# Four transformer layers on one core: a new dispatcher that decides per engine, and layer-norm roots as a power on GpSimd

## The chip, the cores and the metric

The kernel runs on one core of a Trainium2 chip. The metric is the device time of one execution in microseconds (us). The core has five engines with a program each: PE (TensorE, matmuls), DVE (VectorE), ACT (ScalarE), POOL (GpSimd) and SP (SyncE, which here only issues transfers). Each engine runs its own program strictly in order and waits on semaphores for the others, so an instruction that waits also holds everything that stands behind it on its engine.

## What is computed

Two sequences (batch 2) of 1024 tokens with 256 features go through four layers, each with its own weights. All layers have the same skeleton; `_ln` is a layer norm without learned shift, and `mod` stands for the shift, scale and gate vectors that a conditioning vector gives.

```python
h = _ln(x) * (1 + scale) + shift          # layer norm 1 of 3
x = x + gate * (self_attention(h) @ W_o)  # 16 heads of 16
h = _ln(x) * (1 + scale) + shift          # 2 of 3 (in L1 a plain _ln, and no gate)
x = x + gate * (cross_attention(h, context) @ W_co)   # 77 context tokens
h = _ln(x) * (1 + scale) + shift          # 3 of 3
x = x + gate * mlp(h)                     # 256 -> 1024 -> 256
...
def _ln(x):
    m = x.mean(-1, keepdims=True)
    v = ((x - m) ** 2).mean(-1, keepdims=True)
    return (x - m) * jax.lax.rsqrt(v + EPS)
```

L0 has a mask over all 1024 x 1024 scores, L1 and L3 attend to all tokens, L2 attends in windows of 128 tokens and, in its cross attention, keeps only the 16 highest scores of the 77 (top-k). The MLP of L2 is a SwiGLU, the others are GELUs.

## The kernel before

Tokens are held in blocks of 512 (two per sequence), heads in groups. Scores of a query tile go through the PSUM ring `ring_a` (2 places) for their row maximum, which DVE takes, and are then computed again, transposed, in `ring_b` (3 places) for the exponential, which ACT takes; `ring_c` holds the products with V. Intermediate tensors travel through DRAM (`scr_q`, `scr_k`, `scr_out`, `scr_recip`).

The order of all work is fixed before the program is built. `plan()` describes the work as some dozens of coroutines ("threads") that ask for steps with `do(kind, ph, ...)`. `ph` lists the step's phases, an engine and an assumed duration each, for instance PE and then DVE; `lat` is the assumed latency of a transfer. A thread has a rank (tables `RANK`, `SECOND`, `LATER`), buffers are handed out by `Slots`, and `LINK` is the assumed time of a hand-over. `Plan.run` repeatedly takes the step that can begin first, or one of lower rank that could begin within `REACH` of it or would be wanted soon on a later phase's engine (`YIELD`). `emit` then books all phases of the step at once, each behind what has already been booked on its engine. The list `p.steps`, in the order of booking, is the order of the programs of SP, ACT, DVE and POOL. For PE alone, `play` goes through the list a second time and makes an order of its own, `pe_order`, and in a third pass it puts numbers of filling matmuls into the places where it expects PE to wait.

Those fills are products of an identity matrix with 256 columns that nothing reads (L1318 and L1322). Their number is the expected wait in us, less a margin, times 0.8 (L1318) or 0.7 (L1322), divided by `FILL_ONE` = 0.11.

A layer norm of one block is the steps `stats` and `norm` on DVE and two steps `turn` (PE transposes at L1336, ACT writes `h_feat` at L1570). `stats` is four BN_STATS (L1672), four BN_AGGR (L1675) and `inverse_root` (L1635 to L1645): fourteen operations on 128x4 numbers, each waiting for the one ahead. `norm` is four TENSOR_SCALAR (L1682) into `x_norm`, of which there is one buffer. There are 48 of them: 4 layers of 3, for 2 sequences of 2 blocks. POOL splits the row maxima into three bf16 parts (L1882 to L1885) and sends them to the query ring (L1890), prepares the top-k exponents (L1896 to L1899), multiplies gates into weights (L1864) and adds biases to the residual (L1874).

## Time and profile before

| | us |
|---|---|
| median of 3 runs (3001.68 to 3004.83) | 3004.18 |
| span of the profiled execution, first to last instruction | 3001.3 |
| PE busy, filling matmuls included | 2791.8 |
| DVE busy | 2002.4 |
| ACT busy | 1400.1 |
| POOL busy | 638.6 |

The span is that of one profiled execution; it lies within the range of the three runs, and 2.9 us below their median. Busy time is the time in which an engine had at least one instruction under way. A matmul's busy time is its latency, so the times of single groups on PE overlap at their edges and add up to more than PE's. The kernel's line numbers are written L1322.

### The profile page before, as it was taken

What the parts mean: (1) busy time and instruction counts of PE and PEld (TensorE: products, weight loads), DVE (VectorE), ACT (ScalarE), POOL (GpSimd) and SP (SyncE); (2) the same over time, 40 slices, a digit from 0 to 9 for tenths busy, and PEclk for the clock granted to TensorE, in tenths of its full rate; (3) what the DMA queues carried; (4) which work ended last, traced back from release to release, by engine and by line L of the source; (5) the groups of instructions that cost most, each with busy time, mean ns of one, the idle gap of its engine ahead of it and who ended that gap; (6) DMA issues with size and microseconds to landing.
All of it is one profiled execution on the core that took longest, in us unless ns stands there. A gap on an engine that the chain in (4) does not pass through costs nothing.

```text
span 3001.3 us, 48815 instructions
## 1 busy us (share of the span) xinstructions
PE 2791.8 (93%) x15447; PEld 1384.9 (46%) x15447; DVE 2002.4 (67%) x4848; ACT 1400.1 (47%) x2571; POOL 638.6 (21%) x967
## 2 busy tenths in 40 slices
PE   8999999999999998999988888889799999999899
PEld 5533344335536324334465566666553433333556
DVE  7778387643683865884355669677888694886631
ACT  3255635663453663664635233322225355577341
POOL 2010011221410110131124435424321000112220
PEclk9999999999999999999999999999999999999899
DMA  7323122322551312243166415531232042123521
GB/s 208 103 66 121 47 64 78 107 66 85 155 164 41 92 50 75 68 131 94 40 191 184 132 49 175 155 89 35 94 103 57 15 128 51 44 58 100 180 92 37
DMA packets 268160, 286.87 MB, mean 96 GB/s; under 512 B 70665, under 2 KB 207243, under 8 KB 267275
## 3 DMA queue, kind: packets, MB, share of 16 engines
q1 hardware_dynamic: 256651, 282.28, 32.0%
q8 instruction: 136, 2.23, 0.3%
q0 software_dynamic: 11264, 1.46, 0.3%
q14 instruction: 109, 0.89, 0.1%
HBM read 167.43 MB, written 114.72 MB: 94 GB/s over the span
## 4 chain that ended last, share of the span: by engine, by line
PE 68%; DVE 13%; issue 7%; DMA 5%; POOL 2%; ACT 2%; SPq 2%; DVEq 0%; ACTq 0%; POOLq 0%
PE ring_c L1491 11%; PE ring_b L1458 11%; PE ring_a L1414 10%; PE ring_a L1526 7%; PE ring_b L1514 6%; PE ring_b L1457 4%; PE ring_a L1503 3%; PE ring_b L1371 3%; DVE row_max L1776 2%; PE ring_a L1514 1%; DMA reciprocals<-scr_recip 1%; PE ring_a L1386 1%; DMA q_ring<-neg_max_parts 1%; PE ring_b L1485 1%; PE ring_b L1336 1%
## 5 line engine op out<-in xcount | busy, mean ns | idle before, releaser
L1599 ACT ACTIVATE probs<-ring_b 128x512 f32<-128x512 f32 (+1 forms) x1728 | 904.8, 604 | 498.0 <-PE ring_b L1458 434.8
L1776 DVE TENSOR_REDUCE row_max<-ring_a 128x1 f32<-128x1024 f32 x512 | 600.1, 1219 | 130.5 <-PE ring_a L1414 127.6
L1458 PE MATMUL ring_b<-q_ring,k_ring 100*128 100x512 bf16 x1536 | 514.0, 381 | 20.9 <-ACT probs L1599 4.8
L1414 PE MATMUL ring_a<-k_ring,q_ring 96*128 96x512 bf16 x1536 | 450.8, 383 | 21.0 <-issue 3.8
L1491 PE MATMUL ring_c<-probs,v_and_ones 128*17 128x512 f32 x3072 | 400.9, 599 | 5.3 <-ACT probs L1599 4.8
L1882 POOL CAST neg_max_parts<-neg_max 16x128 bf16<-16x128 f32 x112 | 33.0, 294 | 1594.7 <-ACT neg_max L1593 1265.6
L1773 DVE CUSTOM_DVE_ANT_0 w_mlp<-ring_a,w_mlp 128x1024 bf16<-128x1024 f32 x256 | 300.6, 1221 | 53.2 <-PE ring_a L1414 52.6
L1820 DVE TENSOR_TENSOR x_tok<-x_tok,ring_a 128x512 f32<-128x512 f32 x96 | 66.0, 688 | 338.8 <-PE ring_a L1526 206.7
L1458 PEld LDWEIGHTS ring_b<-q_ring,k_ring 100*128 100x128 bf16 x1536 | 142.2, 97 | 313.3 <-issue 210.1
L1414 PEld LDWEIGHTS ring_a<-k_ring,q_ring 96*128 96x128 bf16 x1536 | 127.6, 98 | 298.8 <-issue 219.9
L1514 PE MATMUL ring_b<-h_feat,w_mlp 128*128 128x512 f32 x512 | 229.9, 597 | 3.6 <-ACT h_feat L1570 1.7
L1526 PE MATMUL ring_a<-w_mlp 128*128 128x256 f32 x1024 | 225.6, 381 | 3.1 <-issue 1.9
L1526 PEld LDWEIGHTS ring_a<-w_mlp 128*128 128x128 f32 x1024 | 194.0, 191 | 34.3 <-issue 8.3
L1457 PE MATMUL ring_b<-w_mlp 128*128 128x512 bf16 x512 | 194.4, 380 | 0.7 <-issue 0.4
L1617 ACT ACTIVATE w_mlp<-ring_b,bias_cols 128x512 f32<-128x512 f32 x128 | 87.9, 687 | 200.5 <-PE ring_b L1514 200.4
L1890 POOL DMA_DIRECT2D q_ring<-neg_max_parts x336 | 166.4, 499 | 38.1 <-POOL neg_max_parts L1885 29.8
L1779 DVE TENSOR_REDUCE row_max<-ring_a 128x8 f32<-128x616 f32 (+1 forms) x128 | 111.0, 901 | 80.1 <-PE ring_a L1424 62.0
L1583 ACT ACTIVATE raw<-ring_b,bias_cols 128x512 f32<-128x512 f32 (+1 forms) x104 | 69.1, 664 | 180.7 <-PE ring_b L1371 165.8
L1514 PEld LDWEIGHTS ring_b<-h_feat,w_mlp 128*128 128x128 f32 x512 | 96.0, 191 | 120.7 <-issue 110.8
L1593 ACT ACTIVATE neg_max<-ring_b 16x128 f32<-16x128 f32 x112 | 29.0, 260 | 244.1 <-PE ring_b L1439 244.0
L1570 ACT ACTIVATE h_feat<-ring_b,mod_cols 128x512 f32<-128x512 f32 (+1 forms) x92 | 66.3, 757 | 141.4 <-PE ring_b L1336 141.0
L1896 POOL TENSOR_SCALAR topk_marks<-topk_marks 128x616 f32<-128x616 f32 x32 | 72.6, 2269 | 272.0 <-DVE topk_marks L1801 271.7
(149 smaller groups left out, 3726.7 us busy)
## 6 DMA issues: line engine op xcount, KB each, us to landing
q_ring<-scr_q SPq DMA_DIRECT2D x128, 384.0 KB, 4.4
scr_q<-split SPq DMA_DIRECT2D x64, 384.0 KB, 2.9
k_ring<-scr_k SPq DMA_DIRECT2D x64, 384.0 KB, 5.2
scr_q<-split SPq DMA_DIRECT2D x64, 256.0 KB, 3.1
scr_out<-out_stage SPq DMA_DIRECT2D x128, 128.0 KB, 2.6
scr_out<-out_stage SPq DMA_DIRECT2D x64, 256.0 KB, 2.2
h_feat<-scr_out SPq DMA_DIRECT2D x56, 256.0 KB
reciprocals<-scr_recip SPq DMA_DIRECT2D x56, 256.0 KB
```

The costliest lines, as they stand in the source:

```text
L1371: last = mm(ps[:, 0:s.width], w[:, k, at + s.hh * P:at + (s.hh + 1) * P], src[:, k, 0:s.width], start=k == 0, stop=k == KF - 1)
L1414: last = mm(ps[:, half * BLOCK:(half + 1) * BLOCK], q[0:PARTS, h, t * P:(t + 1) * P], k_view(g)[0:PARTS, h, half * BLOCK:(half + 1) * BLOC ...
L1457: mm(ps[:, :], IDB[:], MASKT[:, s.kt, q0:q0 + BLOCK], start=True, stop=False)
L1458: last = mm(ps[:, :], k_view(g)[0:ROWS, h, s.kt * P:(s.kt + 1) * P], q[0:ROWS, h, q0:q0 + BLOCK], start=not g.masked, stop=True)
L1491: last = mm(rows, VA[:, u.kt, g.heads[tile % 2], :], probs, start=u.kt == 0, stop=u.last)
L1514: last = mm(ps[:, 0:BLOCK], w1[:, k, at:at + P], HT[:, k, s.b, s.blk * BLOCK:(s.blk + 1) * BLOCK], start=k == 0, stop=k == KF - 1)
L1526: last = mm(ps[:, t * FEAT:(t + 1) * FEAT], HID[:, k, tok:tok + P], W2[:, k, :], start=k == 0, stop=k == HIDDEN // P - 1)
L1599: f(PT[0:n, s.pt, :], ps[0:n, :], ACT.Exp, **kw).then_inc(b_evac, 1)
L1773: v.tensor_tensor_reduce(out=JUNK[:, k, :], in0=ps, in1=MASKQ[:, t, :], scale=1.0, scalar=-3.4e38, op0=ALU.add, op1=ALU.max, accum_out=NM[ ...
L1776: v.tensor_reduce(NM[:, s.nm, s.u:s.u + 1], ps, AX.X, ALU.max).then_inc(a_evac, 1)
L1779: v.tensor_reduce(NM[:, s.nm, s.u * 8:s.u * 8 + 8], ps.rearrange("p (i k) -> p i k", k=P)[:, :, 0:n], AX.X, ALU.max).then_inc(a_evac, 1)
L1890: pool.dma_start(QR[PARTS + 1 + j:PARTS + 2 + j, g.q, :], MS[:, s.ms, j, :]).then_inc(max_in[g.q], 16)
```

## The change

`Plan.run` now treats phases one by one. A step's first phase is a candidate, and so is the head of each of three queues of later phases (`a` and `b` for the rings, `c` for the rest). The engine whose candidate can begin first is chosen, and on it the candidate of lowest rank that can begin within `REACH`, which is now at most 0.2. `issue` books one phase and appends the step to `order[engine]`, so each engine, PE too, has an order of its own from one pass, and the fills are set in that pass by the formulas of before. `play`, `YIELD` and `emit` are gone. Nearly all assumed durations and latencies are new numbers, as are `RANK`, `SECOND`, `LATER`, `REACH` and `LINK`, and after a pair of PE steps of different kind around `pv` a little is added. Buffers go round in the order in which they are given back, and a step that gives one back has no assumed early time any more.

A layer norm has a step more. DVE does the statistics and signals (`stats_ready`); POOL does `root`, an addition of eps and a power of -0.5 on 128x4 numbers; DVE's `norm` waits for `root_ready`. The one root for the context tokens (77x2, once in the program) stays on DVE with its Newton steps. POOL now also waits for DVE's constants before its first instruction.

```diff
-LINK = dict(PE=0.22, ACT=0.16, DVE=0.13, POOL=0.12, SP=0.1)
+LINK = dict(PE=0.31, ACT=0.14, DVE=0.13, POOL=0.1, SP=0.0)
...
-            first, head = min(((at, t) for at, t in ready), key=lambda x: (x[0], x[1].rank))
-            eng = head.want["ph"][0][0]
-            at, t = min(((at, t) for at, t in ready if t.want["ph"][0][0] == eng and at <= first + REACH[eng]),
-                        key=lambda x: (x[1].rank, x[0]))
...
+            for q in self.queue.values():
+                if q:
+                    s, n, at = q[0]
+                    eng = s["ph"][n][0]
+                    ready.append((max(at, self.free[eng]), s["rank"], 0, None, s, n, eng))
...
+            at, _, _, _, _, _, eng = min(ready, key=lambda x: x[:3])
+            at, rank, _, t, s, n, _ = min((x for x in ready if x[6] == eng and x[0] <= at + REACH[eng]), key=lambda x: x[1:3] + x[:1])
...
-REACH = dict(PE=0.05, ACT=0.25, DVE=1.2, POOL=5, SP=0.1)
+REACH = dict(PE=0.0, ACT=0.1, DVE=0.0, POOL=0.2, SP=0.2)
...
-            s = yield do("stats", [("DVE", 4.7)], after=[src], l=l, i=i, b=b, blk=blk, src=src)
+            s = yield do("stats", [("DVE", 1.85)], after=[src], counts=["stat_n"], l=l, i=i, b=b, blk=blk, src=src)
+            s = yield do("root", [("POOL", 1.0)], after=[s], counts=["root_n"], l=l, i=i, b=b, blk=blk, of=s)
             xn, last, _ = yield ("get", "XN")
-            n = yield do("norm", [("DVE", 1.9)], after=[s, last], counts=["xn_n"], l=l, i=i, b=b, blk=blk, xs=xn, last=last)
+            n = yield do("norm", [("DVE", 1.293)], after=[s, last], counts=["xn_n"], l=l, i=i, b=b, blk=blk, xs=xn, last=last,
+                         root=s)
...
-            s = yield do("mod", [("PE", 1.75), ("DVE", 0.55)], after=[s], ring="a", l=l, i=i, n=n)
+            s = yield do("mod", [("PE", 1.68), ("DVE", 0.41)], after=[s], ring="a", l=l, i=i, n=n)
...
-                    link(last)
-                    inverse_root(RSTD[:, s.b, s.blk, 0, :], RSTD[:, s.b, s.blk, 1, :], mv[:, :, 1], LAYERS[s.l]["eps"])
+                    last.then_inc(stats_ready, 1)
                 elif s.kind == "norm":
                     if s.last is not None:
                         dve.wait_ge(b_full, s.last.bn + 1)
+                    dve.wait_ge(root_ready, s.root.root_n + 1)
...
+            pool.wait_ge(setup_dve, 1)
+            for s in whole.order["POOL"]:
...
+                elif s.kind == "root":
+                    pool.wait_ge(stats_ready, s.of.stat_n + 1)
+                    y = RSTD[:, s.b, s.blk, 0, :]
+                    link(g_.tensor_scalar(RSTD[:, s.b, s.blk, 1, :], MV[:, s.b, s.blk, :, 1], LAYERS[s.l]["eps"], None, ALU.add))
+                    g_.tensor_tensor(out=y, in0=RSTD[:, s.b, s.blk, 1, :], in1=HALF[:], op=ALU.pow).then_inc(root_ready, 1)
+                    pool.wait_ge(root_ready, s.root_n + 1)
```

Where the change moves instructions, three places show it. The first is DVE in layer L2, in the middle of the top-k (MAX and MATCH_REPLACE find the sixteen highest scores of `topk_scores`, `x_tok` is the residual). Before, the rows from one `x_norm` to the next top-k are:

```order
L1682 TENSOR_SCALAR x_norm<-x_tok,mean_var,rstd 128x256 x4
L1672 BN_STATS bn_stats<-x_tok 128x6 x4
L1675 BN_AGGR mean_var<-bn_stats 128x2 x4
L1637 TENSOR_SCALAR mean_var<-mean_var 128x4
L1638 COPY rstd<-mean_var 128x4
L1639 TENSOR_SCALAR rstd<-rstd 128x4
L1640 TENSOR_TENSOR rstd<-root_seed,rstd 128x4
L1641 TENSOR_SCALAR mean_var<-mean_var 128x4
L1643 TENSOR_TENSOR rstd<-rstd 128x4
L1644 TENSOR_TENSOR rstd<-rstd,mean_var 128x4
L1645 SCALAR_TENSOR_TENSOR rstd<-rstd 128x4
```

Two more rounds of the last three rows follow there, then the next MAX. At the like place of the changed kernel, still on DVE in L2, there is:

```order
L1764 MATCH_REPLACE topk_marks<-topk_next,topk_marks 128x77 x8
L1635 BN_STATS bn_stats<-x_tok 128x6 x4
L1638 BN_AGGR mean_var<-bn_stats 128x2 x4
L1783 TENSOR_TENSOR x_tok<-x_tok,ring_a 128x512
L1645 TENSOR_SCALAR x_norm<-x_tok,mean_var,rstd 128x256 x4
L1783 TENSOR_TENSOR x_tok<-x_tok,ring_a 128x512
```

The fourteen operations are gone, and one residual addition stands between the statistics and the `x_norm` that now needs POOL's answer. In the whole program the changed DVE order has at most two short operations or one residual pair (under 1.4 us at the mean durations of the groups of before) between the two at 22 of the 48 places, nothing at all at nine of these, and more at 26.

The second place is POOL in L2 (`neg_max_parts` are the split maxima, `topk_marks` the top-k exponents). Before:

```order
L1864 TENSOR_TENSOR w_mlp<-w_mlp,gate 128x2048
L1868 TENSOR_TENSOR gate<-gate,row_biases 128x256
L1896 TENSOR_SCALAR topk_marks<-topk_marks 128x616
L1898 TENSOR_TENSOR topk_scores<-topk_scores,topk_first 128x616
L1899 TENSOR_TENSOR topk_scores<-topk_scores,topk_marks 128x616
```

And in the changed kernel:

```order
L1828 TENSOR_TENSOR w_mlp<-w_mlp,gate 128x2048
L1838 TENSOR_TENSOR gate<-gate,row_biases 128x256
L1844 TENSOR_TENSOR x_tok<-x_tok,gate 128x1024
L1833 TENSOR_SCALAR rstd<-mean_var 128x4
L1834 TENSOR_TENSOR rstd<-rstd,minus_half 128x4
L1866 TENSOR_SCALAR topk_marks<-topk_marks 128x616
L1868 TENSOR_TENSOR topk_scores<-topk_scores,topk_first 128x616
L1869 TENSOR_TENSOR topk_scores<-topk_scores,topk_marks 128x616
```

The root stands behind a bias addition, which itself waits for an `x_norm`, and ahead of a top-k. Of the 48 roots, 11 stand right behind a bias addition, 5 right behind a top-k, 15 right behind DMA issues of the maxima, and 14 right behind another root.

The third place is PE at the start of the program (`ident_f` alone are the fills). Before:

```order
L1329 MATMUL ring_a<-cond,w_mod_or_cross_kv 128x2 x8
L1322 MATMUL ring_b<-ident_f 128x256 x46
L1336 MATMUL ring_b<-ident_f,x_norm 128x128 x8
L1322 MATMUL ring_b<-ident_f 128x256 x6
L1371 MATMUL ring_b<-h_feat,w_qkv 128x512 x2
```

And after:

```order
L1291 MATMUL ring_a<-cond,w_mod_or_cross_kv 128x2 x8
L1284 MATMUL ring_b<-ident_f 128x256 x11
L1298 MATMUL ring_b<-ident_f,x_norm 128x128 x8
L1284 MATMUL ring_b<-ident_f 128x256 x6
L1333 MATMUL ring_b<-h_feat,w_qkv 128x512 x4
```

The planner puts 11 fills instead of 46 ahead of the first transpose. Over the whole program the fills go from 2071 to 1873: 1083 to 1013 between L2's first window scores and its last top-k transpose, 652 to 633 ahead of that, 336 to 227 behind it. All other matmuls are the same in number and shape.

## Rows read from the trace of the kernel before

**Rows 1.** The page: span, busy time of each engine

```profile
span 3001.3 us, 48815 instructions
PE 2791.8 (93%) x15447; PEld 1384.9 (46%) x15447; DVE 2002.4 (67%) x4848; ACT 1400.1 (47%) x2571; POOL 638.6 (21%) x967
```

**Rows 2.** Three stretches: length, busy of PE, PEld, DVE, ACT, POOL; clock, DMA

```profile
0.00:1500.00 1500.00, 1425.69 (x7551) 626.22 (x7552) 982.68 (x1824) 782.21 (x1446) 246.12 (x449) 0.99 0.32 93
1500.00:2200.00 700.00, 601.24 (x3986) 415.75 (x3986) 500.27 (x2185) 223.55 (x384) 277.85 (x284) 0.94 0.43 125
2200.00:3000.00 800.00, 764.83 (x3912) 342.90 (x3910) 519.44 (x839) 394.32 (x741) 114.64 (x235) 0.99 0.25 75
```

**Rows 3.** Fills alone, sums over 0 to 3000: L1322, then L1318

```profile
sum 3000.00, PE 170.51 PEld 130.39; mean PE 56.84 PEld 43.46
sum 3000.00, PE 120.55 PEld 75.21; mean PE 40.18 PEld 25.07
```

**Rows 4.** The chain that ended last, share of the span by engine

```profile
PE 68%; DVE 13%; issue 7%; DMA 5%; POOL 2%; ACT 2%; SPq 2%; DVEq 0%; ACTq 0%; POOLq 0%
```

**Rows 5.** PE's waits: in total, times, longest

```profile
PE ring_b L1336 <- DVE x_norm L1682: 25.2, 12, 4.7
```

**Rows 6.** DVE's groups of the roots: busy, mean ns | idle before

```profile
L1637 DVE TENSOR_SCALAR mean_var<-mean_var 128x4 f32<-128x4 f32 x48 | 16.9, 352 | 1.6
L1638 DVE COPY rstd<-mean_var 128x4 f32<-128x4 f32 x48 | 8.7, 182 | 1.6
L1639 DVE TENSOR_SCALAR rstd<-rstd 128x4 int32<-128x4 int32 x48 | 14.2, 297 | 1.6
L1640 DVE TENSOR_TENSOR rstd<-root_seed,rstd 128x4 int32<-128x4 int32 x48 | 8.3, 174 | 1.6
L1641 DVE TENSOR_SCALAR mean_var<-mean_var 128x4 f32<-128x4 f32 x48 | 9.9, 206 | 1.6
L1643 DVE TENSOR_TENSOR rstd<-rstd 128x4 f32<-128x4 f32 x144 | 23.7, 164 | 4.9
L1644 DVE TENSOR_TENSOR rstd<-rstd,mean_var 128x4 f32<-128x4 f32 x144 | 23.7, 165 | 5.0
L1645 DVE SCALAR_TENSOR_TENSOR rstd<-rstd 128x4 f32<-128x4 f32 x144 | 23.5, 163 | 4.9
```

**Rows 7.** The chain again, in time: first root on it, one of L2

```profile
794.17 0.18 DVE mean_var L1637
...
797.25 1.39 DVE x_norm L1682 x4
...
2154.28 2.96 DVE mean_var L1637
...
2160.25 0.81 DVE topk_scores L1785
```

**Rows 8.** Timeline around the second of them: start, length, instruction

```profile
2152.69 4.52 POOL L1864 TENSOR_TENSOR w_mlp<-w_mlp,gate 128x2048 f32<-128x2048 f32 x1 [9.23 <-DVE gate L1704]
2154.28 2.95 DVE L1637 TENSOR_SCALAR mean_var<-mean_var 128x4 f32<-128x4 f32 x1
```

**Rows 9.** POOL's groups: busy, mean ns | idle before

```profile
L1896 POOL TENSOR_SCALAR topk_marks<-topk_marks 128x616 f32<-128x616 f32 x32 | 72.6, 2269 | 272.0 <-DVE topk_marks L1801 271.7
L1874 POOL TENSOR_TENSOR x_tok<-x_tok,gate 128x1024 f32<-128x1024 f32 x24 | 57.6, 2400 | 76.0 <-DVE x_norm L1682 70.5 <-ACT probs L1599 4.7
L1899 POOL TENSOR_TENSOR topk_scores<-topk_scores,topk_marks 128x616 f32<-128x616 f32 x32 | 49.1, 1535 | 2.5
L1883 POOL TENSOR_TENSOR neg_max<-neg_max,neg_max_parts 16x128 f32<-16x128 f32 x112 | 48.8, 436 | 9.4
L1898 POOL TENSOR_TENSOR topk_scores<-topk_scores,topk_first 128x616 f32<-128x616 f32 x32 | 40.7, 1272 | 2.7
L1852 POOL TENSOR_SCALAR kv_mask_col<-topk_scores 77x2 f32<-77x2 uint8 x1 | 0.5, 506 | 0.1
```

**Rows 10.** VectorE's largest constant, by the same columns

```profile
L1647 DVE MEMSET v_and_ones<- 128x2176 f32 x1 | 1.9, 1872 | 1.3 <-PEq L1986 1.3
```

510 lines of the change are left out of this document (236 added, 274 removed).

## Prediction

> **What bounds the kernel now.** I read the page first: TensorE is busy for 2791.8 of 3001.3 us, VectorE for two thirds, ScalarE for under half, GpSimd for a fifth [rows 1]. But TensorE's figure holds filling matmuls that nothing reads, so the second view is the fills alone: 170.5 us at L1322 and 120.5 us at L1318, 291 us in all [rows 3]. With the 209.5 us in which TensorE is idle (3001.3 less 2791.8), 500 us of the span are not work of TensorE. The necessary matmuls, some 2500 us, are the same before and after. All that this change can win or lose on TensorE lies in those 500 us: they are what the order of steps costs.
>
> The third view, three stretches of the span, tells where they are. Layers L0 and L1 (0 to 1500 us) leave TensorE idle for 74 us, L2 (1500 to 2200) for 99 of 700, L3 for 35 of 800. The granted clock falls to 0.94 of full speed in L2 and is 0.99 elsewhere [rows 2]. L2 also holds 142 of the 291 us of fills (122.0 and 20.3 in the same windows), so nearly half of the 500 us lies in the top-k layer, where VectorE is busy for 500 of 700 us and GpSimd is at its busiest. The fourth view, the chain that ended last, says the same: 68% TensorE, but 13% VectorE and 5% transfers [rows 4]. And in the list of waits, TensorE's largest single cause of idle is `x_norm`, the result of a layer norm: 25.2 us in 12 waits, up to 4.7 us each [rows 5].
>
> **The roots.** The change takes eight groups of operations from VectorE. Their busy time is 16.9+8.7+14.2+8.3+9.9+23.7+23.7+23.5 = 128.9 us, and the idle ahead of them, which is one operation waiting for the last, adds 22.8 us [rows 6]: 152 us for 48 roots, 3.2 us each. Most of that lies beside TensorE work and gives nothing. What counts is how many are on the chain. Walking it from start to end I find eleven of the 48, the first at 794.17 us and the longest at 2154.28 us [rows 7]. The first takes 3.08 us (794.17 to 797.25), the longest 5.97 us (to 2160.25). The eleven take 37.9 us of operations and about 3 us between them, 41 us. Seven of them are in L2.
>
> The longest is worth a look, because it shows a cost that is in no group's name: L1637, an operation on four numbers per partition, took 2.95 us, and ended within 0.05 us of the end of a GpSimd multiplication of 4.52 us that had begun ahead of it [rows 8]. VectorE was held by GpSimd. The mean of L1637 is 352 ns where its neighbours need about 165 [rows 6]. The Trainium skill (SBUF — State Buffer, "Who interferes with whom") says that a VectorE operation in a two-port mode and a GpSimd operation exclude each other for the whole instruction; the trace agrees, with the 2.95 us above. By that rule the root loses a way to be blocked on VectorE and wins one on GpSimd.
>
> In their place come two GpSimd instructions on 128x4 numbers and two hand-overs. The trace has no power operation. From below, the nearest rows are the small ones: 436 ns for 16x128, 506 ns for a TENSOR_SCALAR on two numbers per partition [rows 9], so 0.9 us for both and about 0.3 us for the hand-overs, 1.2 us. From above I take for the power what GpSimd needs for 616 elements, 2269 ns [rows 9]: 3 us in all. I take 1.2 us, as four elements per lane are much nearer to the small rows. Eleven roots then cost 13 us, not 41: 28 us less at best. As the new chain will partly run through something that was just behind, I take 25 us; the bounds are 41 (all hidden behind the VectorE work that now stands between statistics and `x_norm`) and 8 (3 us each).
>
> A rule speaks against the move: the Trainium skill (GPSIMD Engine Reference, "Engine selection") sends elementwise work to VectorE, since GpSimd is about twice as slow on two inputs. The rows show 436 ns against 165 ns per instruction, which is in that direction; but two instructions replace fourteen, so the rule would be decisive only if the power took over 2 us.
>
> **The order.** It can't be priced from a row, since every engine's order is another. What can be counted are the fills, since each stands for a wait that the planner expects, by the same formulas in both kernels. They go from 2071 to 1873, 198 fewer. At 291.06 us / 2071 = 0.1405 us each, that is 28 us. Turned back through the formulas, a fill stands for 0.11/0.8 to 0.11/0.7 us of expected wait, 0.138 to 0.157 us: 27 to 31 us. I take 29 us. This is what the new planner expects of a program with longer hand-overs from TensorE (0.31, not 0.22), so it is not flattered by optimistic links. The saving is 109 fills behind the top-k, 70 in it and 19 ahead.
>
> Part of this is the saving of the roots seen twice, because the old planner booked 4.7 us of VectorE for what is now 1.85 and a GpSimd step. I put the overlap at 15 us. Against it stand the 209.5 us of idle that no fill covers. The old formulas expect 2071 x 0.147 = 304 us of waits, while fills and idle together are 500 us: some 195 us of what TensorE loses was not foreseen. A booking that lets an engine take a later phase in a gap, and hand-overs and transfers priced anew, should get some of it back. I take 15 us; the bounds are a gain of 100 (half of it) and a loss of 60, since a new order has new collisions.
>
> **The sum.** 25 + 29 - 15 + 15 = 54 us less than the span of 3001.3: 2947. The median of the runs is 2.9 us above that span, so the forecast is 2950 us.
>
> What is added elsewhere is nothing at this scale: one memset of four numbers on VectorE, and GpSimd's wait for VectorE's constants ahead of its own, in the first microseconds, when the first transposes are still behind a load of x. The longest of VectorE's constants takes 1.87 us [rows 10]; if that cover were gone, that is about what it would cost, once.
>
> **The rivals.**
>
> *A queue on GpSimd holds `x_norm` (slower).* GpSimd works in order. Five roots stand right behind a top-k group of 2.27+1.27+1.54 = 5.1 us, eleven behind a bias addition of 2.4 us [rows 9] that itself waits for another block's `x_norm`. At 22 of 48 places VectorE has less than 1.4 us to do between statistics and `x_norm`, so a late root stops VectorE, then the score maxima behind it, then TensorE through `ring_a`. It decides when the wait at those 22 exceeds the assumed 1.2 us by 54/22 = 2.5 us. With an excess of 4 us at all of them it is 88 - 54 = 34 us slower: about 3038. For it speaks L2, with GpSimd busy for 278 of 700 us [rows 2]; against it, that GpSimd is idle for 60% even there, and that the planner knows the queue. 17%.
>
> *The order does not hold (no change).* Static orders are as good as their durations. If the unforeseen idle grows by as much as the planned waits shrink, the time is 2998 to 3010. For it speaks that the place of most loss, the top-k, keeps its 1013 fills; against it, that the root's saving doesn't hang on the order. 8%, and another 8% for a gain of under 20 us.
>
> *The order gains much more.* If half of the 195 us of unforeseen waits go, the time is 2860 to 2900. For it speaks that TensorE's clock in L2 (0.94) would rise with fewer holes; 700 x 0.05 = 35 us is the bound of that alone. 17%.
>
> *GpSimd has to fetch code for the power.* The Trainium skill (GPSIMD Engine Reference, "Instruction dispatch") has about 6 us for the first call of a freshly loaded function. No row here shows it, and once in a program it would change nothing. As a mechanism of this kernel, a switch between multiplication and power that costs as much as the longest GpSimd instruction in the trace, 4.5 us [rows 8], at each of the eleven roots on the chain gives 11 x 4.5 = 50 us back: no change, 3000. 3%, counted in the 8% of no change.
>
> **How the numbers follow.** My case, a gain of 20 to 90 us, has 50%: 2914 to 2984. Much more gain 17%, little gain 8%, no change 8%, slower 17%. Faster by over 0.2% is 75%, within 0.2% (about what a measurement of this kernel can tell from no change) 8%, slower 17%. For 8 in 10 I cut the outer half of each tail: 2875 to 3035.
>
> **What would show it.** Right: VectorE's busy time falls by about 129 us to some 1875; the two GpSimd groups have means near 0.3 to 0.6 us; fills at 1873; idle of TensorE under 200 us; the wait of the transposes on `x_norm` under 25 us; the clock in L2 at 0.95 or more. Wrong: a power operation of over 2 us; VectorE's `x_norm` with more than 50 us of idle ahead of it put down to GpSimd; idle of TensorE over 250 us.

## The result and the profile after

| | before | changed kernel |
|---|---|---|
| median | 3003.59 us (3001.68 to 3004.83, 4 runs) | 2984.93 us (2978.93 to 2988.23, 4 runs) |
| ratio | | 0.9942 [0.9925, 0.996] |

Once more on another chip the ratio was 0.9933 [0.9911, 0.9955]. The change makes the kernel 0.6% faster, 19 us. I had forecast 54 us: the sign and the range held the result, the size did not, and the rest of this text is about the missing 35 us.

The page of the changed kernel, its span and the busy time of each engine (the line numbers of the changed kernel are 37 or 38 lower than before for TensorE, VectorE and ScalarE, 30 lower for GpSimd):

```profile
span 2985.6 us, 47850 instructions
PE 2766.4 (93%) x15193; PEld 1377.7 (46%) x15249; DVE 1892.3 (63%) x4177; ACT 1421.3 (48%) x2579; POOL 714.7 (24%) x1063
```

Three stretches, with the columns of [rows 2]; then the two fills alone, as in [rows 3], L1280 first:

```profile
0.00:1500.00 1500.00, 1413.65 (x7460) 631.77 (x7517) 934.65 (x1517) 782.50 (x1439) 279.31 (x493) 0.98 0.32 93
1500.00:2200.00 700.00, 604.48 (x3918) 408.08 (x3918) 479.83 (x2001) 234.40 (x397) 300.95 (x314) 0.92 0.44 128
2200.00:2980.00 780.00, 746.73 (x3813) 336.82 (x3811) 477.11 (x659) 404.44 (x743) 134.40 (x257) 0.98 0.25 73
...
sum 2980.00, PE 145.34 PEld 102.11; mean PE 48.45 PEld 34.04
...
sum 2980.00, PE 117.14 PEld 84.06; mean PE 39.05 PEld 28.02
```

The fills fell from 291.1 to 262.5 us, 28.6 less, as forecast. But TensorE is now idle for 2985.6 - 2766.4 = 219.2 us, 9.7 more than before [rows 1], and its necessary work takes 2503.9 us instead of 2500.7. So of 28.6 us of fills, 15.7 us came out as time between the two profiled executions. Some matmul records are missing from this trace: 56 of the 512 at L1419 (15193 matmuls stand against 15249 weight loads, while the kernel before has 15447 of both). The idle time found beside them adds up to 3.8 us, so of the 9.7 us between 6 and 9.7 are real. The granted clock is a little lower too: 0.92 in L2 where it was 0.94, and 0.98 elsewhere where it was 0.99 [rows 2].

The groups of the new root and of what waits for it (busy, mean ns | idle before):

```profile
L1833 POOL TENSOR_SCALAR rstd<-mean_var 128x4 f32<-128x4 f32 x48 | 11.7, 243 | 435.5 <-DVE mean_var L1638 434.5
L1834 POOL TENSOR_TENSOR rstd<-rstd,minus_half 128x4 f32<-128x4 f32 x48 | 50.6, 1054 | 4.0
L1645 DVE TENSOR_SCALAR x_norm<-x_tok,mean_var,rstd 128x256 f32<-128x256 f32 x192 | 81.2, 485 | 32.6 <-POOL rstd L1834 23.7 <-PE ring_b L1298 8.6
```

The power takes 1.05 us and the addition 0.24, 1.3 us together, where the prediction had 0.9 us for the two. With both hand-overs it is some 1.6 us from the end of the statistics to `x_norm` at 12 of the 16 places where VectorE waits for it, against the 1.2 us assumed. VectorE waits 23.7 us in all; GpSimd idles 434.5 us ahead of the roots, so it is mostly free when they come. The chain that ended last and VectorE's waits for transfers (in total, times, longest) show where more was lost:

```profile
PE 69%; DVE 12%; DMA 9%; issue 5%; POOL 2%; SPq 2%; ACT 1%; DVEq 0%; ACTq 0%; POOLq 0%
...
DVE h_feat L1777 <- DMA reciprocals<-scr_recip: 112.1, 32, 14.8
...
DVE denominators L1771 <- DMA denominators<-scr_out: 31.5, 9, 16.8
```

The same waits of the kernel before:

```profile
DVE h_feat L1814 <- DMA reciprocals<-scr_recip: 66.4, 15, 8.7
...
DVE denominators L1808 <- DMA denominators<-scr_out: 11.2, 4, 5.0
```

VectorE's share of the chain fell by a point, that of transfers rose from 5% [rows 4] to 9%. The waits are those of one round trip, by which the attention's result is divided by its softmax sums: the result goes to DRAM (`scr_out`), the sums come back (`denominators`), VectorE inverts them, they go out again (`scr_recip`), come back spread over the heads (`reciprocals`), and VectorE multiplies (`h_feat`, L1777). VectorE waits 66 us longer in it than before.

### The profile page after: what moved, and what is told of

Read it like the earlier page. It is cut to its first block, busy times and chain, and to the rows that moved or that the text cites. A ratio compares the mean times of both kernels' runs of the same rounds, so it can differ in the third digit from the quotient of the medians.

```text
span 2985.6 us, 47850 instructions
## 1 busy us (share of the span) xinstructions
PE 2766.4 (93%) x15193; PEld 1377.7 (46%) x15249; DVE 1892.3 (63%) x4177; ACT 1421.3 (48%) x2579; POOL 714.7 (24%) x1063
## 4 chain that ended last, share of the span: by engine, by line
PE 69%; DVE 12%; DMA 9%; issue 5%; POOL 2%; SPq 2%; ACT 1%; DVEq 0%; ACTq 0%; POOLq 0%
PE ring_b L1420 11%; PE ring_c L1453 11%; PE ring_a L1376 10%; PE ring_b L1476 7%; PE ring_a L1488 7%; PE ring_b L1419 3%; PE ring_b L1333 3%; PE ring_a L1465 3%; DVE row_max L1739 2%; PE ring_a L1476 2%; DMA reciprocals<-scr_recip 2%; PE ring_b L1447 1%; DMA scr_out<-out_stage 1%; PE ring_a L1348 1%; PE ring_b L1408 1%
## 5 line engine op out<-in xcount | busy, mean ns | idle before, releaser
L1561 ACT ACTIVATE probs<-ring_b 128x512 f32<-128x512 f32 (+1 forms) x1728 | 919.2, 599 | 443.8 <-PE ring_b L1420 355.4
L1420 PE MATMUL ring_b<-q_ring,k_ring 100*128 100x512 bf16 x1536 | 528.1, 381 | 15.0 <-ACT probs L1561 2.0
L1376 PEld LDWEIGHTS ring_a<-k_ring,q_ring 96*128 96x128 bf16 x1536 | 136.1, 98 | 252.3 <-issue 148.8
L1419 PE MATMUL ring_b<-w_mlp 128*128 128x512 bf16 x456 | 173.3, 380 | 0.3 <-issue 0.2
L1465 PE MATMUL ring_a<-w_out,h_feat 128*128 128x256 f32 x512 | 130.9, 409 | 11.0 <-DVE h_feat L1777 5.4
L1333 PE MATMUL ring_b<-h_feat,w_qkv 128*128 128x512 f32 x256 | 128.9, 631 | 1.1 <-issue 0.9
```

The lines of the kernel that those rows point to most:

```text
L1333: last = mm(ps[:, 0:s.width], w[:, k, at + s.hh * P:at + (s.hh + 1) * P], src[:, k, 0:s.width], start=k == 0, stop=k == KF - 1)
L1376: last = mm(ps[:, half * BLOCK:(half + 1) * BLOCK], q[0:PARTS, h, t * P:(t + 1) * P], k_view(g)[0:PARTS, h, half * BLOCK:(half + 1) * BLOC ...
L1419: mm(ps[:, :], IDB[:], MASKT[:, s.kt, q0:q0 + BLOCK], start=True, stop=False)
L1420: last = mm(ps[:, :], k_view(g)[0:ROWS, h, s.kt * P:(s.kt + 1) * P], q[0:ROWS, h, q0:q0 + BLOCK], start=not g.masked, stop=True)
L1465: last = mm(ps[:, t * FEAT:(t + 1) * FEAT], HT[:, k, s.b, tok:tok + P], WO[:, s.wo.slot, k, :], start=k == 0, stop=k == KF - 1)
L1561: f(PT[0:n, s.pt, :], ps[0:n, :], ACT.Exp, **kw).then_inc(b_evac, 1)
```

## The experiments

Each median stands beside its ratio to the kernel before on the same chip. "Old orders" are those of the kernel before, "new orders" those of the changed kernel. The expectations name theories by letters. A: the new root no longer costs anything, and the missing gain is lost because the new orders are laid out as if every transfer landed in its usual time. B, its rival: the missing gain is in the root's new path over GpSimd. C: transfers cost both kernels alike. D and G, which came later, are A at one place: the round trip of the reciprocals, and the weight load that holds its store. E, F, H, I and J are the rivals of single runs.

### What a root is worth in either order

Both kernels with the root left out, a linear formula of the variance in its place:

```diff
-                    inverse_root(RSTD[:, s.b, s.blk, 0, :], RSTD[:, s.b, s.blk, 1, :], mv[:, :, 1], LAYERS[s.l]["eps"])
+                    link(v.tensor_scalar(RSTD[:, s.b, s.blk, 0, :], mv[:, :, 1], 1.0e-6, 0.25, ALU.mult, ALU.add))
```

> The kernel before with every engine's order untouched; in place of the fourteen operations of a root VectorE makes one (variance times a millionth plus 0.25), so the root is left out of the computation. It bounds what the roots cost in the old order. My prediction's term (eleven roots on the chain, 41 us, 28 us net of their successors): 20 to 35 us less than before, 2968 to 2984. Rival, roots mostly beside other work and what is behind them just as late: under 10 us less, over 2994.

> The changed kernel with every order untouched except that GpSimd's two instructions of a root are gone: VectorE makes one operation (variance times a millionth plus 0.25, so the root is left out) and signals itself. It bounds what the root still costs in the new order. Theory A (the gain went into transfers and hand-overs that the new plan expects too early): at most 12 us less than the changed kernel, 2972 to 2985. Theory B (the roots on GpSimd hold x_norm on VectorE, 23.7 us of waits, and the maxima behind them on GpSimd, 69 us of waits): 20 to 40 us less, 2945 to 2965.

Measured: old orders 2977.9 us, ratio 0.9931 [0.9905, 0.9957]; new orders 2984.14 us, 0.995 [0.9931, 0.9969]. In the old orders the roots cost 23 us; in the new ones what is left of them costs nothing that these runs can tell (2984.1 against 2984.9 us). Theory B is refuted.

Then the root alone changed, with the orders kept: on GpSimd in the old orders (at the place where GpSimd finds `stats` in the list), and back on VectorE in the new ones.

```diff
+                elif s.kind == "stats":
+                    pool.wait_ge(stats_ready, s.stat_n + 1)
...
+                    g_.tensor_tensor(out=y, in0=RSTD[:, s.b, s.blk, 1, :], in1=HALF[:], op=ALU.pow).then_inc(root_ready, 1)
```

> The kernel before with all its orders kept, but the fourteen operations of a root replaced by GpSimd's addition and power, at the place that the old list of steps gives the statistics, and x_norm waiting for it. Nothing else of the change. The bound with no root at all was 2978. If the roots alone carry the whole gain of the change: 2978 to 2990, as fast as the changed kernel (2985) or faster. If GpSimd's queue, for which this order was not made, holds x_norm: over 2995.

> The changed kernel with all its orders kept, but the root back on VectorE with its fourteen operations right behind the statistics; GpSimd has none. This is the new dispatcher, its tables and its order without the moved root. Theory A, the new order gives nothing by itself: 3000 to 3020, no faster than before (3001). Had the order a gain of its own, as my prediction's 29 us, it would be at 2960 to 2985.

Measured: 2995.8 us, 0.9976 [0.9965, 0.9987], and 3066.93 us, 1.0218 [1.02, 1.0236]. So there is a table:

| median, us | root on VectorE | root on GpSimd | no root |
|---|---|---|---|
| old orders | 3003.6 | 2995.8 | 2977.9 |
| new orders | 3066.9 | 2984.9 | 2984.1 |

The old orders ask for `x_norm` right behind the statistics, so there GpSimd's answer is waited for, in 18 places, and 6 to 8 of 23 us are won (the run with GpSimd's root in the old orders):

```profile
DVE x_norm L1685 <- POOL rstd L1874: 30.0, 18, 5.6
```

The new orders give the answer time; with VectorE's long root back in them the kernel is 82 us slower, far above both ranges that I had expected. The two halves of the change need each other. But with no root in either, the new orders are not better than the old ones: 2984 against 2978 us (the intervals of the two ratios overlap). All of the 29 us that I had put down to the order is missing.

### The new planner by itself

The changed kernel planned anew for a root on VectorE (`stats` booked at 4.6 us, no `root` step):

```diff
-            s = yield do("stats", [("DVE", 1.85)], after=[src], counts=["stat_n"], l=l, i=i, b=b, blk=blk, src=src)
-            s = yield do("root", [("POOL", 1.0)], after=[s], counts=["root_n"], l=l, i=i, b=b, blk=blk, of=s)
+            s = yield do("stats", [("DVE", 4.6)], after=[src], counts=["stat_n"], l=l, i=i, b=b, blk=blk, src=src)
```

> The new dispatcher and all its tables, planned anew for a root on VectorE (statistics booked at 4.6 us, no step on GpSimd); every order differs from that of the changed kernel, and its fills rise from 1873 to 2310. If a rank table serves any program about as well: 2995 to 3015. If the table fits only the one program it was found for: over 3030.

Measured: 3054.46 us, 1.0176 [1.016, 1.0191]. The new dispatcher, left to plan for the old root, makes a kernel 53 us slower than the old one does. Its ranks are those of the changed kernel, so this is the second case of the expectation, a table that fits only its own program, and no verdict on the dispatcher. And the changed kernel with margins on its assumed times:

```diff
+        us *= SLOW
...
-        s["end"] = end + s.get("lat", 0.0)
+        s["end"] = end + s.get("lat", 0.0) * FAR
...
+FAR, SLOW = 1.15, 1.02
```

> The changed kernel with the margins of the old second pass put into the new planner: transfers booked at 1.15 times their latency, engines at 1.02 times their durations, which moves every order and gives 2105 fills. If the new plan loses because it expects transfers too early, and margins cure it: 2960 to 2980. If the rank table is fitted to its own assumptions, and any change of them costs more than the margins give: over 3000.

Measured: 3003.31 us, 1.0013 [0.9997, 1.0028]; transfers fell to 6% of the chain, while "issue" rose to 8%:

```profile
PE 69%; DVE 12%; issue 8%; DMA 6%; POOL 2%; ACT 2%; SPq 1%; DVEq 0%; ACTq 0%; POOLq 0%
```

This, too, came out as the expectation's second case has it. The run changed two things at once, the margin and how well the ranks fit, and says nothing on the first.

### What the fills are worth

No fills, with either order:

```diff
-                if s.get("fill_o"):
+                if False:
...
-                if s.get("fill"):
+                if False:
```

> The changed kernel without its 1873 filling matmuls, nothing else touched. If fills stand only where TensorE waits anyway, the time moves by under 10 us, but for the clock: mean granted clock below 0.95 and 10 to 40 us more. If fills stand in the way of work, because the waits fell elsewhere than planned: 5 to 25 us less.

> The same for the kernel before, its 2071 fills left out. By theory A the old plan's waits came where they were expected more often, so its fills are in the way of less: it loses at least as much as the changed kernel loses without its own, 10 to 50 us more than 3004. If both move alike, fills tell nothing on the difference.

Measured: new orders 3003.46 us, 1.0002 [0.9985, 1.0019]; old orders 3055.48 us, 1.0185 [1.0163, 1.0208]. The fills are worth 52 to 55 us in the kernel before and 18 to 22 in the changed one. Their pages (new orders first, then old):

```profile
span 3008.0 us, 44160 instructions
PE 2657.7 (88%) x13376; PEld 1226.5 (41%) x13376; DVE 1895.8 (63%) x4177; ACT 1422.3 (47%) x2579; POOL 711.7 (24%) x1063
```

```profile
span 3052.8 us, 44673 instructions
PE 2685.5 (88%) x13376; PEld 1229.8 (40%) x13376; DVE 2006.4 (66%) x4848; ACT 1401.9 (46%) x2571; POOL 639.5 (21%) x967
```

Without fills the necessary matmuls take 2657.7 and 2685.5 us instead of some 2500, at mean clocks of 0.919 and 0.913 of full speed instead of 0.967 and 0.978. The fills are not mere place-holders for waits: they buy back some 150 to 185 us of TensorE's own work. A count of fills therefore prices nothing by itself. Fills plus idle is nearer to it: 500.6 us before, 481.7 us after, 18.9 us less, of which the other matmuls took 3.2 us back. That leaves the 15.7 us between the profiled executions; the medians are 18.7 us apart. Without fills the changed kernel is ahead by 52 us, with them by 19: the old orders have more to gain from fills. How much of that lies in where the fills stand, these runs do not tell.

### Where the chain got longer

Loads of the query and key rings with half of their rows (half of each dot product is left out):

```diff
-                    sp.dma_start(q_view(g)[0:PARTS], QK_SCR["q"][g.b, h0:h0 + len(g.heads), :, :, t0:t0 + g.span]
+                    sp.wait_ge(ones_ready, 2)
+                    sp.dma_start(q_view(g)[0:PARTS // 2], QK_SCR["q"][g.b, h0:h0 + len(g.heads), 0:HEAD // 2, :, t0:t0 + g.span]
```

> The kernel before with its orders as they are; each load of the q ring and of the k ring carries half of its rows (8 of 16 elements of each head), and the other rows are zeroed once at the start, so the scores leave out half of each dot product. What is asked: how much of the time hangs on these transfers. Theory A (the orders of the changed kernel are laid out as if each transfer landed in its usual time, those of the kernel before as if it took longer, so the latter can bear late transfers): the kernel before gains little, 0 to 10 us, so 2992 to 3004 us, ratio 0.996 to 1.0. Rival C (late transfers cost both kernels alike, and the missing gain lies elsewhere): it gains as much as the changed kernel does with the same edit, within 5 us.

> The changed kernel with the same edit: loads of the q ring and the k ring carry half of their rows, the others are zeroed once, half of each dot product is left out. Theory A: its DMA share of the chain (9%) shrinks towards the 5% of before and PE's waits for the q ring and for what comes after it shrink, and it gains 15 to 30 us: 2955 to 2970 us, ratio to the kernel before 0.984 to 0.989. Rival C: it gains the same as the kernel before does, within 5 us. If neither gains anything, the latency of these loads lies in fixed parts and not in their bytes, and the theory is not tested by this pair.

Measured: 2985.9 us, 0.9957 [0.994, 0.9973], and 2964.76 us, 0.9882 [0.9867, 0.9898]: 13 to 16 us and 18 to 20 us. The difference of 2 to 7 us is no verdict between theories A and C: the old orders gained more than the 0 to 10 us that theory A gave them, and these loads cost both kernels nearly alike.

Then the round trip of the reciprocals left out (the division by the softmax sum is replaced by a constant factor; VectorE's operations stay):

```diff
                 elif s.kind == "recip_put":
+                    continue
...
                 elif s.kind == "recip_get":
+                    continue
...
-                    dve.wait_ge(rb_in[s.got.e], s.got.need)
```

> The kernel before with its orders as they are; the reciprocals of the attention's denominators are still computed by VectorE, but are neither stored to DRAM nor read back spread over the heads: h_feat is multiplied by a constant set once at the start. So SP issues two kinds of transfers less and VectorE's h_feat no longer waits for them (66.4 us in 15 waits in the kernel before). The division by the softmax sum is left out. Theory D (what the new orders lose, they lose on VectorE behind this round trip, which is planned at its usual time): the kernel before gains 5 to 20 us, 2983 to 2998 us, ratio 0.994 to 0.998. Rival C (transfers cost both kernels alike): it gains as much as the changed kernel does by the same edit, within 5 us.

> The changed kernel with the same edit; the division by the softmax sum is left out. In the changed kernel VectorE waits 112.1 us in 32 waits for this round trip, up to 14.8 us each. Theory D: it gains 35 to 60 us, to 2925 to 2950 us, ratio to the kernel before 0.974 to 0.983, and DMA's share of the chain falls from 9% to 5% or less. Rival C: it gains what the kernel before gains, within 5 us. A third outcome, neither gains 5 us, would say that these waits of VectorE are slack, however long they look.

Measured: old orders 2991.77 us, 0.9965 [0.9951, 0.9978]; new orders 2945.44 us, 0.9814 [0.98, 0.9829]. The same edit is worth 8 to 10 us before and 36 to 40 us after. Without the trip the two kernels differ by 46 us, near the 54 forecast: some 28 of the missing 35 us hang on this one path. The changed kernel without the trip shows what came back (the busy times of its page, and its L2 stretch with the columns of [rows 2]):

```profile
PE 2737.5 (93%) x15193; PEld 1361.2 (46%) x15249; DVE 1892.6 (64%) x4178; ACT 1420.6 (48%) x2579; POOL 712.0 (24%) x1063
...
1500.00:2200.00 700.00, 613.30 (x4024) 410.82 (x4023) 501.07 (x2028) 239.40 (x402) 309.89 (x323) 0.96 0.40 118
```

Its span is 2940.0 us, 45.6 less. Only 16.8 us of them are idle of TensorE (202.4 instead of 219.2). The other 28.9 are TensorE's busy time (2737.5 instead of 2766.4), with fewer than 5 us of it in the fills: the granted clock in L2 rose from 0.92 to 0.96, and over the span from 0.967 to 0.980. So more than half of what the trip costs the changed kernel is paid through a slower TensorE, not as idle. Leaving out the fills and leaving out the trip both bring the distance of the two kernels back to some 50 us; these worths can't be added.

The chain says the same of the path, walked from start to end in both kernels. Before, the four kinds of transfer of the trip (`scr_out`, `denominators`, `scr_recip`, `reciprocals`) are 60 us in 13 pieces; after, 141 us in 27. All transfers together are 165 and 254 us of the chains. The longest of the seven stores of reciprocals on the changed kernel's chain, with its neighbours (start, length):

```profile
1921.22 0.39 SPq L1114
1921.62 0.04 issue
1921.66 10.06 DMA scr_recip<-denominators
1931.74 0.59 SPq L1241
```

A store of 32 KB takes 10 us here. L1114, which the same queue issued 0.44 us ahead of it, is a load of 2 MB of MLP weights. The timeline of the same place (start, length, engine):

```profile
1921.22 0.39 SPq L1114 DMA_DIRECT2D w_mlp<-in_w  x1
1921.66 0.47 SPq L1232 DMA_DIRECT2D scr_recip<-denominators  x1
...
1931.74 1.23 SPq L1241 DMA_DIRECT2D reciprocals<-scr_recip  x2
...
1935.53 0.69 DVE L1777 TENSOR_TENSOR h_feat<-h_feat,reciprocals 128x512 f32<-128x512 f32 x1 [14.79 <-DMA reciprocals<-scr_recip]
```

VectorE stands for 14.79 us. The time from the issue of this store to that of its read-back is 3.91 us on average over 48 places, 3.21 before; three of the 48 are near 10 us, each 0.4 to 3.1 us behind a weight load, and the longest of the kernel before is 8.2. At all six stores that stand within 4 us behind a load of MLP weights this time is 5.3 to 10.1 us, at the other 42 its median is 3.05. But at one of those 42 it is 8.2 us, so a weight load is not the only thing that lengthens it.

### Asking later, and letting the weights wait

In the first of two edits on VectorE's order, 13 of the 64 multiplications are moved behind one to four row maxima that stood behind them; in the second, 22 are moved:

```diff
+    dve_order = whole.order["DVE"]
+    late = {428: 4, 448: 2, 592: 2, 593: 2, 681: 2, 702: 2, 742: 2, 743: 2, 795: 1, 825: 2, 1401: 3, 1416: 2, 1422: 2}
+    for at in sorted(late, reverse=True):
...
+        dve_order.insert(at + late[at], dve_order.pop(at))
```

> The changed kernel, whose VectorE order is changed in 13 of 64 places only: a multiplication by the reciprocals (h_feat), behind which up to four row maxima of score tiles stand, is moved behind one to four of them. Nothing else is moved, no work is added or left out. In the changed kernel VectorE waits at these 13 for 43 us in all, while the scores may already lie in ring_a. Theory D (the order asks for the reciprocals before they are back): of the 43 us some 25 can be filled, VectorE's h_feat waits for the reciprocals fall from 112.1 to about 85 us, and the time falls by 5 to 15 us, to 2970 to 2980 us, ratio 0.989 to 0.993. Rival E (the row maxima have nothing to do there, since the round trip holds all engines at a change of layers): no gain, 2982 to 2988 us. Rival F (the multiplication is late for TensorE's output projection): slower, 2990 to 3000 us.

> The changed kernel with 22 of the 64 multiplications moved (13 of the run before, two of them now behind five row maxima, and nine that had stood ahead of a root's end, a reciprocal, a split, a gate or an up2). Nothing else is changed. Theory D: what is left of VectorE's waits for the reciprocals (78 us) lies where the layer changes and only other reciprocals and one or two steps can be put ahead; they fall to about 65 us and the time by 0 to 6 us more than in the run before: ratio 0.989 to 0.992. Rival F (late multiplications hold TensorE's output projection): above the run before by 3 us or more, ratio over 0.993.

> The changed kernel once more, as it is, on the same chip as its variants, so that they are compared without the spread between chips. Expected is its ratio to the kernel before of 0.994 again (0.9925 to 0.996); the variant with moved multiplications stays under it by 0.002 to 0.005.

Measured: 2972.64 us, 0.992 [0.9899, 0.9941]; 2974.74 us, 0.9913 [0.9894, 0.9933]; and the changed kernel as it is, on the chip of the second, 2981.57 us, 0.9933 [0.9911, 0.9955]. By the ratios each variant is 4 to 9 us faster than the changed kernel in one or the other of its two measurements, and on the same chip the second is 7 us faster. The intervals of the ratios overlap, so a gain is likely, as two variants agree, but not clear of noise. VectorE's waits fell to 78.3 and to 40.7 us (the second variant):

```profile
DVE h_feat L1782 <- DMA reciprocals<-scr_recip: 40.7, 19, 7.5
```

Two thirds of the wait are gone, but at most a third of the 28 us. That VectorE asks too early is a small part; the trip itself is on the chain (119 us of it in the second variant, 141 in the changed kernel).

The last edit lets five of the weight loads (with rows and gates beside them) stand behind the read-back:

```diff
+    for at, behind in ((379, 382), (380, 382), (442, 447), (443, 447), (444, 447), (459, 461), (621, 628), (622, 628), (632, 637)):
...
+        moved.setdefault(behind, []).append(at)
```

> The changed kernel with SP's order changed at five places: loads of MLP weights (w_mlp, 1 or 2 MB, issued 0.4 to 3.1 us ahead of a store of reciprocals) with the rows and gates beside them stand behind the read-back of those reciprocals instead. Nothing else is moved. At these five the time from the issue of the store to the issue of the read-back, which waits for the store, is 6.3, 5.3, 10.1, 9.9 and 7.7 us, against 3.5 us at the median of 48. Theory G (what holds the round trip is the weight load ahead of it in the same queue): the five fall to 3 to 5 us each, VectorE's waits for the reciprocals by 10 to 20 us, and the time by 4 to 15 us, to 2967 to 2978 us, ratio 0.988 to 0.992. Rival H (the store is held by something else, the DMA traffic of the layer's change): the five stay above 5 us and the time is 0.993 to 0.996. Rival I (the weights come late instead): the five fall but the time rises by up to 10 us, PE or POOL waits for w_mlp.

Measured: 3004.44 us, 1.0 [0.9985, 1.0016], 20 us slower than the changed kernel. On the store itself theory G is right in the main: the same store now takes 4.0 us to its read-back instead of 10.1. Of the other four, 6.3, 9.9 and 7.7 us became 1.9, 6.9 and 4.3, while 5.3 became 5.1; of the stores that took near 10 us one is left, which was not touched. VectorE's waits for the reciprocals fell from 112.1 to 91.9 us. On the time theory G is refuted. The timeline:

```profile
1924.76 0.46 SPq L1238 DMA_DIRECT2D scr_recip<-denominators  x1
1928.79 1.21 SPq L1247 DMA_DIRECT2D reciprocals<-scr_recip  x2
1930.11 0.39 SPq L1120 DMA_DIRECT2D w_mlp<-in_w  x1
```

The price is rival I's, on another tile than it named: what was moved with the weights comes late. TensorE's waits for `w_gate`, changed kernel first, then this run:

```profile
PE ring_a L1312 <- DMA w_gate<-in_mod: 4.6, 2, 4.1
```

```profile
PE ring_a L1318 <- DMA w_gate<-in_mod: 14.5, 4, 7.7
```

VectorE's waits for the products of the SwiGLU's second half, again both:

```profile
DVE w_mlp L1787 <- PE ring_a L1476: 40.1, 26, 5.0
```

```profile
DVE w_mlp L1793 <- PE ring_a L1482: 50.4, 26, 12.6
```

On the chain, loads of `w_gate` are 25.4 us in three pieces, where the changed kernel has 7.3 us in one, and the trip is 130 us, not 141: what the trip gave back, `w_gate` took. In these places the new orders want the trip and the weights at the same time, from one queue, and putting the one behind the other moved the wait without ending it. That this is all of the 20 us is not shown.

### Other ranks

The last pair keeps the changed kernel and its dispatcher and has other ranks for the threads, `REACH` and `DELAY` (a start time) with them, found by a random search. Both book the root at 1.32 us. In the first, transfers are booked at 1.3 times their time, and a plan is judged by carrying out its fixed orders with transfers that last 15 to 30% longer and queue; in the control it is judged by its own assumed times:

```diff
-RANK = dict(
...
+FAR, SLOW = 1.3, 1
...
-            s = yield do("root", [("POOL", 1.0)], after=[s], counts=["root_n"], l=l, i=i, b=b, blk=blk, of=s)
+            s = yield do("root", [("POOL", 1.32)], after=[s], counts=["root_n"], l=l, i=i, b=b, blk=blk, of=s)
```

(In the control `FAR` is 1.0.)

> The changed kernel with new ranks (RANK, SECOND, LATER, DELAY, REACH) and 1927 fills. The ranks come from a random search which judged each plan by carrying out its fixed orders with transfers that take 15% or 30% longer than assumed and queue behind one another, and all transfers are booked at 1.3 times their time. Everything else is the changed kernel's. Theory D, G (what is missing hangs on transfers that the plan takes too lightly): 2940 to 2970 us, ratio 0.979 to 0.989, and below the control run. Rival J (this way of judging is no nearer to the chip than the plan's own times): 2980 to 3010 us, no better than the changed kernel's 2982 to 2985 us or than the control.

> The control: ranks from an equally long search by the same moves, which judged each plan by its own assumed times, with transfers as short as the changed kernel has them; 1670 fills instead of 1873. By its own times this is the best of all plans. Theory D, G: its gain is in waits that come back on the chip, so it is no faster than the changed kernel: 2980 to 3020 us, ratio 0.993 to 1.006, idle of TensorE above 219 us, transfers 8% of the chain or more. Rival J: it is faster than the changed kernel by 10 us or more, under 2972 us, and no slower than the run with long transfers.

Measured: 2945.61 us, 0.9805 [0.979, 0.982], and the control 2937.64 us, 0.9798 [0.9776, 0.9819]. Both are some 2% faster than the kernel before and 39 to 47 us faster than the changed kernel (41 and 43 by the ratios), and the control is no worse: what theories D and G expected of it is refuted, and rival J holds. The pages' second lines and the chains (long transfers first):

```profile
PE 2750.3 (93%) x15248; PEld 1372.1 (47%) x15303; DVE 1883.2 (64%) x4177; ACT 1417.8 (48%) x2575; POOL 708.0 (24%) x1063
...
PE 73%; DVE 12%; issue 6%; DMA 4%; POOL 3%; ACT 2%; SPq 0%; DVEq 0%; ACTq 0%; POOLq 0%
```

```profile
PE 2720.5 (93%) x14990; PEld 1342.9 (46%) x15046; DVE 1879.4 (64%) x4177; ACT 1424.6 (49%) x2581; POOL 710.3 (24%) x1063
...
PE 67%; DVE 13%; issue 9%; DMA 7%; POOL 2%; SPq 1%; ACT 1%; DVEq 0%; ACTq 0%; POOLq 0%
```

| us | before | changed | long transfers | control |
|---|---|---|---|---|
| span | 3001.3 | 2985.6 | 2943.4 | 2934.3 |
| fills | 291.1 | 262.5 | 262.5 | 229.9 |
| idle of TensorE | 209.5 | 219.2 | 193.1 | 213.8 |
| fills plus idle | 500.6 | 481.7 | 455.6 | 443.7 |
| necessary matmuls | 2500.7 | 2503.9 | 2487.8 | 2490.6 |
| transfers on the chain | 165 | 254 | 118 | 215 |
| of these the round trip | 60 | 141 | 54 | 137 |

The three traces of the new dispatcher lack 55 or 56 matmul records each, so their idle is too high by up to 4 us against the kernel before. The last two kernels' necessary matmuls are some 10 to 13 us shorter than before, at a granted clock that is a little lower (0.976 and 0.974, not 0.978); so this line is not the clock alone. Some of it is those missing records, and some how far matmuls and fills overlap, since it is a difference of busy times.

The search with long transfers did what it was asked to: the trip is back to 54 us of the chain and transfers to 4%. It did not end long stores, though. One is on its chain too, and the last load of MLP weights ahead of it was issued 257 us earlier. Loads of the query and key rings stand 2 to 4 us ahead of it; whether they held it was not tested:

```profile
1139.71 9.05 DMA scr_recip<-denominators
```

The control leaves the trip at 137 us and VectorE's wait for it where it was, and wins as much with fewer fills in other places:

```profile
DVE h_feat L1760 <- DMA reciprocals<-scr_recip: 110.8, 27, 15.0
```

So the round trip is where this one order lost its gain, and not what every order by such times has to lose. Whether the control would gain another 30 us without the trip was not run.

## Why the prediction was wrong

**What bounds the kernel.** Half right: fills plus idle fell by 18.9 us, near the gain. But the rest is not the same before and after, as the prediction had it: TensorE's other work took 3.2 us more, and 2480 instead of 2504 us once the trip was left out, at a higher clock. Right too that `x_norm` was a wait of TensorE, but it still is: 25.2 us in 12 before [rows 5], now

```profile
PE ring_b L1298 <- DVE x_norm L1645: 26.4, 15, 4.1
```

**The roots, 25 us.** The size was right: with no root the old orders gain 23 us, and in the new orders the root on GpSimd costs nothing that can be told. The new root was priced too low, 1.2 us for what takes 1.6 with its hand-overs. The prediction also wrote that this saving doesn't hang on the order. It does: in the old orders only 6 to 8 of 25 us come.

**The fills, 29 us.** This step is the one that failed: a fall in planned waits was booked as saved time, us for us. The fills did fall by 28.6 us, but with the roots left out of both kernels the new orders are worth nothing (2984.1 against 2977.9 us). "Each stands for a wait that the planner expects" is a statement on the plan. The plan books a transfer for its usual time wherever it stands in the queue, so the waits of TensorE that it no longer fills are partly still there: 6 to 9.7 us more idle, and a lower clock (0.967, not 0.978). TensorE's waits for loads of the query ring grew from 7.8 to 19.3 us, those for the top-k exponentials from 12.5 to 21.3. The roots' 23 us and nothing for the order is about the 19 us measured. Where it went is shown for the most part: some 28 us hang on the round trip. Why this order and not the control's, with the same trip on its chain, loses by it stays open.

**The overlap (-15) and the unforeseen waits (+15).** The second had the wrong sign. I wrote that hand-overs and transfers priced anew should get some of the 195 us back. The round trip's waits on VectorE grew by 66 us instead and its share of the chain from 60 to 141 us. The view that would have told was there: the prediction named 5% of transfers on the chain and did not ask which transfers, or what the new SP order puts ahead of them.

**The signs.** Of those named for "right", VectorE's busy time fell by 110 us instead of 129, the power is at 1.05 us instead of 0.3 to 0.6, idle of TensorE is at 219 us instead of under 200, the wait on `x_norm` at 26.4 us instead of under 25, and the clock in L2 at 0.92 instead of 0.95. None of those named for "wrong" came.

**The rivals.** "The order does not hold" was given 8%, and 8% more for a gain under 20 us; that was the right mechanism, what was not foreseen growing as planned waits shrink. The queue on GpSimd did not happen (23.7 us of waits, 434.5 us of GpSimd's idle ahead of the roots). Neither did a fetch of code: the power's mean over 48 is 1.05 us, its first call took 1.04, and all 48 have 4.0 us of idle ahead of them together. The hold of VectorE by GpSimd, for which the prediction named the rule of the Trainium skill (SBUF — State Buffer, "Who interferes with whom"), can't have cost the roots more than the 23 us that all of them cost. An estimate from [rows 6]: L1637 took 16.9 us where L1641, an operation of the same form, took 9.9, so 7 us of busy time on this line. On the chain it is 7.7 us in its eleven places, where it would be 2.3 at the mean of L1641: some 5 us of the 23.

## What to carry to other kernels

A new static order is worth what fills plus idle fall by and what happens to the busy time of the rest, not what the count of planned fills falls by. List the transfers on the chain by kind before and after: here the small stores of a round trip took 5 to 10 us right behind a weight load, and 3 us at the median elsewhere. And one table of ranks is one draw: with the same dispatcher and the same assumed times, but for the root's, other ranks gave 43 to 47 us more, so a scheduler is not to be judged by a single order. Where a latency is shortened and an order is made anew together, run the four corners: here the halves were worth 8 us and minus 63 us apart and 19 us together.

## What was not expected of the hardware

- GpSimd's power on 128x4 numbers takes 1.05 us, its addition on as many 0.24 us; the first call is as short as the others (one of the 48 took 1.60).
- Fills of 291 us take 52 us off the time, and 262 us of them in another order only 18 to 22: the granted clock goes from 0.913 to 0.978 in the first and from 0.919 to 0.967 in the second. Whether that is due to where the fills stand was not tested.
- A store of 32 KB took 10.06 us behind a weight load of 2 MB in the same queue, and 4.0 us to its read-back when the load stood behind it (one place each). In another order of the same program a store of reciprocals took 9.05 us with no load of MLP weights near.
- Leaving out a round trip through DRAM gave TensorE 28.9 us of busy time back and only 16.8 us of idle, the granted clock going from 0.967 to 0.980.
